# Queries and keys saved and stacked by halves, and the keys' projection moved ahead of y2's second half

## The reference, cut to what matters

```
x = x + L0(gn(x))      # gn: group norm in 32 groups of 4 channels, no affine
x = x + L1(gn(x))

L0: router: softmax over mean and std of the image -> 2 of 8 experts
    shared = silu(group_norm(conv1x1(x, 8 groups)))
    expert_k = silu(group_norm(conv3x3(x, w[chosen k], 8 groups))) * weight_k
    return shared + expert_1 + expert_2
L1: q, k, v = qkv_w @ x + qkv_b            # per pixel, 128 -> 3 * 128
    windows of 8 x 8 pixels (64 tokens), 8 heads of 16 channels
    attn = softmax(q k^T / 4 + bias[head])
    o = attn @ v + depthwise_conv7x7(v)
    return proj_w @ o + proj_b
```

## Time and profile before

| | |
|---|---|
| median of three runs | 932.93 us |
| the profiled execution | 934.59 us |
| its span | 932.9 us |
| TensorE busy | 743.6 us, 80% |
| VectorE busy | 578.1 us, 62% |
| ScalarE busy | 457.7 us, 49% |
| GpSimd busy | 197.0 us, 21% |
| clock granted to TensorE, mean | 0.879 |

### The profile page before, as it was taken

How to read it: one execution, slowest core, us unless ns; L and a number is a source line. 1 busy time by engine, 2 the same in 40 slices (tenths; PEclk the granted TensorE clock), 3 DMA queues, 4 the chain that set the end, 5 groups by cost and what they waited for, 6 DMA issues and landing times.

```text
span 932.9 us, 18414 instructions
## 1 busy us (share of the span) xinstructions
PE 743.6 (80%) x6926; PEld 422.7 (45%) x6926; DVE 578.1 (62%) x1136; ACT 457.7 (49%) x746; POOL 197.0 (21%) x289
## 2 busy tenths in 40 slices
PE   6143768888888989888989887979797989978785
PEld 5121334454545554545454545454545456534321
DVE  4724456675767666767676757575757587632296
ACT  1204546555555564646464646464646465344422
POOL 3122123131213140403130313131313020000044
PEclk9976969797979797979888988888988989999999
DMA  9224444545464545455554545454546254586435
GB/s 353 106 71 116 139 113 146 145 128 156 144 178 136 163 148 150 150 153 165 142 170 128 173 136 173 123 173 120 177 132 177 67 176 132 161 276 217 156 157 203
DMA packets 84046, 145.29 MB, mean 156 GB/s; under 512 B 24179, under 2 KB 48886, under 8 KB 83958
## 3 DMA queue, kind: packets, MB, share of 16 engines
q1 hardware_dynamic: 58102, 100.89, 34.8%
q0 software_dynamic: 21248, 25.36, 10.9%
q10 hardware_dynamic: 4608, 17.86, 5.2%
HBM read 84.21 MB, written 51.41 MB: 145 GB/s over the span
## 4 chain that ended last, share of the span: by engine, by line
PE 41%; DMA 19%; DVE 16%; ACT 8%; issue 7%; SPq 6%; POOL 1%; POOLq 1%; ACTq 0%; DVEq 0%
PE g L1061 11%; DMA sk_d<-khl 10%; PE g L1057 5%; PE g L1079 4%; PE t L1127 4%; DMA stack<-sk_d 3%; SPq L298 3%; ACT xw L540 3%; PE s L1116 3%; PE pv L1142 3%; DMA vt<-x 3%; PE t L1241 2%; PE s L1112 2%; SPq L292 2%; PE s L1241 2%
## 5 line engine op out<-in xcount | busy, mean ns | idle before, releaser
L806 DVE BATCH_NORM_STATS2 st<-y 128x6 f32<-128x512 f32 x96 | 66.6, 694 | 147.6 <-ACT y L522 147.6
L522 ACT ACTIVATE y<-g 128x512 f32<-128x512 f32 x96 | 57.2, 596 | 167.0 <-PE g L1061 87.0
L1061 PE MATMUL g<-xsh,wsel 96*128 96x512 f32 x256 | 127.8, 627 | 14.0 <-DMA xsh<-xs 10.5
L595 ACT ACTIVATE pt<-t 128x512 f32<-128x512 f32 x128 | 76.2, 597 | 118.8 <-PE t L1127 112.2
L870 DVE TENSOR_REDUCE mx<-s 128x8 f32<-128x512 f32 x128 | 87.8, 686 | 69.6 <-PE s L1116 69.6
L1127 PE MATMUL t<-ident,less 128*128 128x128 f32 x512 | 97.6, 321 | 3.7 <-DVE less L874 3.7
L1142 PE MATMUL pv<-vp,pt 128*64 128x34 f32 x2048 | 95.2, 242 | 5.0 <-ACT pt L595 4.8
L1112 PE MATMUL s<-bias,ident 128*128 128x512 f16 x128 | 56.7, 443 | 52.9 <-DMA stack<-sk_d 52.8
L1142 PEld LDWEIGHTS pv<-vp,pt 128*64 128x64 f32 x2048 | 80.1, 154 | 31.4 <-issue 25.0
L874 DVE TENSOR_TENSOR less<-s,mx 128x512 f32<-128x512 f32 x128 | 88.5, 692 | 4.4
L1079 PE MATMUL g<-xw,w 128*128 128x512 f32 x128 | 66.7, 640 | 15.4 <-ACT y L522 11.7
(11 more groups left out here) (159 smaller groups left out, 1158.5 us busy)
## 6 DMA issues: line engine op xcount, KB each, us to landing
xsh<-xs POOLq DMA_DIRECT2D x64, 210.0 KB, 5.4
stack<-sq_d SPq DMA_DIRECT2D x96, 128.0 KB, 3.1
stack<-sk_d SPq DMA_DIRECT2D x192, 64.0 KB, 2.8
xs<-xn ACTq DMA_DIRECT2D x16, 578.0 KB, 2.9
vt<-x SPq DMA_DIRECT2D x4, 2048.0 KB, 17.7
xin<-x POOLq DMA_DIRECT2D x16, 512.0 KB, 5.8
acc_d<-xr SPq DMA_DIRECT2D x16, 512.0 KB, 5.5
sq_d<-qhl SPq DMA_DIRECT2D x16, 512.0 KB, 7.7
```

The source lines that it names most:

```text
L522: act.activation(y[:, k, h * HALF:(h + 1) * HALF], g[h][:, :], ACT.Identity).then_inc(g_free[h], 1)
L595: act.activation(pt[:, p % 2].rearrange("p i w n -> p (i w n)"), tbk[p % 2][:, :], ACT.Exp).then_inc(sem["exp_done"], 1)
L806: last = v.bn_stats(st[:, 2 * k + h, :], y[:, k, h * HALF:(h + 1) * HALF])
L1061: last = mm(g[h][:, :], wsel[:, k - 1, C * dy:C * dy + C], xsh[:, k - 1, dy + 16 * h:dy + 16 * h + 16, 0:W], start=(dy == 0), stop=(dy == 1))
```

## The change

q and k get a semaphore for each half of the pixels. `save_half` saves one half (256 KB) when its own bank has been read, and for j > 0 when that half's stacks of the image before have landed. `stack_q` and `stack_k` take the place of `stack_qk`; each waits for its own half's save. In a step of SP the order becomes: q saved in two halves, q's first half stacked, k saved in two halves, k's first half stacked; later q's and k's second halves stacked. ScalarE waits by halves before it overwrites qhl and khl. On TensorE, ScalarE, VectorE and in `bank_uses` the keys of image b + 1 at p = 3 now come before y2 (1) of image b + 2; in bank 1 the order becomes q, k, y2 (1).

```diff
@@ bank_uses
         if has1:
             use("q", b + 1)
+        if has1:
+            use("k", b + 1)
         if has2:
             use("y2", b + 2, (1,))
-        if has1:
-            use("k", b + 1)
@@ SP
+            def save_half(j, half, name, dst, src, saved):
+
+                cols = slice(HALF * half, HALF * half + HALF)
+                sp.wait_ge(g_free[half], bank_ready(name, j, half))
+                if j:
+                    sp.wait_ge(stacked[half], STACK * j)
+                sp.dma_start(dst.rearrange("t c n -> c t n")[:, :, cols], src[:, :, cols]).then_inc(saved[half], 16)
+
             def save_q(j):
-
-                sp.wait_ge(g_free[1], bank_ready("q", j, 1))
-                sp.wait_ge(g_free[0], bank_ready("q", j, 0))
+                for half in range(2):
+                    save_half(j, half, "q", sq_d, qhl, q_saved)
+
+            def save_k(j):
+                for half in range(2):
+                    save_half(j, half, "k", sk_d, khl, k_saved)
+
+            def stack_q(j, half):
+
                 if j:
-                    sp.wait_ge(sem["stacked1"], STACK * j)
-                sp.dma_start(sq_d.rearrange("t c n -> c t n"), qhl[:, :, :]).then_inc(sem["q_saved"], 16)
...
+                    sp.wait_ge(sem["s_ready"], PAIRS * (j - 1) + PAIRS // 2 * (half + 1))
+                sp.wait_ge(q_saved[half], 16 * j + 16)
                 cols = slice(HALF * half, HALF * half + HALF)
                 for part, t in enumerate((0, 1, 0)):
                     sp.dma_start(qs[QD * part:QD * part + QD, :, cols],
                                  sq_d[t, :, cols].rearrange("(i c) n -> c i n", i=Q)).then_inc(stacked[half], 16)
+
+            def stack_k(j, half):
+
+                if j:
+                    sp.wait_ge(sem["s_ready"], PAIRS * (j - 1) + PAIRS // 2 * (half + 1))
+                else:
+                    sp.wait_ge(sem["setup_pool"], 1)
+                sp.wait_ge(k_saved[half], 16 * j + 16)
+                cols = slice(HALF * half, HALF * half + HALF)
                 for part, t in enumerate((0, 0, 1)):
...
                 if has1:
                     save_q(b + 1)
+                    stack_q(b + 1, 0)
                     save_k(b + 1)
-                    stack_qk(b + 1, 0)
+                    stack_k(b + 1, 0)
                 if b:
                     save_acc(b - 1)
                 load_x1(b)
                 if has1:
-                    stack_qk(b + 1, 1)
+                    stack_q(b + 1, 1)
+                    stack_k(b + 1, 1)
@@ ScalarE, high_qk
-                act.wait_ge(sem[used], 16 * b)
                 for h in range(2):
+                    act.wait_ge(used[h], 16 * b)
@@ TensorE, step (the same on ScalarE and VectorE)
                     if p == 3:
+                        if has1:
+                            project_qk(b + 1, 1)
                         if has2:
                             convolve(b + 2, 2, (1,))
-                        if has1:
-                            project_qk(b + 1, 1)
```

More of the change, by code:

```diff
@@ L129 @@
 rstd_done coef_scale coef_shift coefs_done silu_done sum_shared sum_first xr_done
-xw_done xr_saved x1_loaded q_hi k_hi q_saved k_saved stacked0 stacked1
+xw_done xr_saved x1_loaded q_hi k_hi q_saved0 q_saved1 k_saved0 k_saved1 stacked0 stacked1
 v_turned v_hi vt_done vt_saved s_ready s_max less_done turned exp_done pv_done
@@ L236, in program @@
         xin_loaded = [sem["xin_loaded0"], sem["xin_loaded1"]]
+        q_saved = [sem["q_saved0"], sem["q_saved1"]]
+        k_saved = [sem["k_saved0"], sem["k_saved1"]]
         stacked = [sem["stacked0"], sem["stacked1"]]
@@ L264, in _ @@
                 sp.dma_start(xall[:, 4 * n:4 * n + 4, :], xb[:, 4 * n:4 * n + 4, :]).then_inc(x_loaded[n], 16)
-            def save_q(j):
-                sp.wait_ge(g_free[1], bank_ready("q", j, 1))
-                sp.wait_ge(g_free[0], bank_ready("q", j, 0))
-                if j:
-                    sp.wait_ge(sem["stacked1"], STACK * j)
-                sp.dma_start(sq_d.rearrange("t c n -> c t n"), qhl[:, :, :]).then_inc(sem["q_saved"], 16)
-            def save_k(j):
[L276 to L284, removed]
+            def save_half(j, half, name, dst, src, saved):
[4 more added lines that the diff above has]
+                sp.dma_start(dst.rearrange("t c n -> c t n")[:, :, cols], src[:, :, cols]).then_inc(saved[half], 16)
+            def save_q(j):
+                for half in range(2):
+                    save_half(j, half, "q", sq_d, qhl, q_saved)
+            def save_k(j):
+                for half in range(2):
+                    save_half(j, half, "k", sk_d, khl, k_saved)
+            def stack_q(j, half):
                 if j:
                     sp.wait_ge(sem["s_ready"], PAIRS * (j - 1) + PAIRS // 2 * (half + 1))
-                elif half == 0:
-                    sp.wait_ge(sem["setup_pool"], 1)
+                sp.wait_ge(q_saved[half], 16 * j + 16)
                 cols = slice(HALF * half, HALF * half + HALF)
@@ L357, in _ @@
             save_k(0)
-            stack_qk(0, 0)
-            stack_qk(0, 1)
+            for half in range(2):
+                stack_q(0, half)
+                stack_k(0, half)
             save_xr(1)
@@ L544, in high_qk @@
             def high_qk(b, n):
-                dst, col, name, used, hi = ((qhl, BQ, "q", "q_saved", "q_hi"), (khl, BK, "k", "k_saved", "k_hi"))[n]
-                act.wait_ge(sem[used], 16 * b)
+                dst, col, name, used, hi = ((qhl, BQ, "q", q_saved, "q_hi"), (khl, BK, "k", k_saved, "k_hi"))[n]
                 for h in range(2):
+                    act.wait_ge(used[h], 16 * b)
                     act.wait_ge(g_ready[h], bank_ready(name, b, h))
@@ L621, in step @@
                     if p == 3:
+                        if has1:
+                            high_qk(b + 1, 1)
                         if has2:
                             copy_y(b + 2, 2, (1,))
-                        if has1:
-                            high_qk(b + 1, 1)
                     if p == 5:
@@ L944, in step @@
                     if p == 3:
+                        if has1:
+                            low_qk(b + 1, 1)
                         if has2:
                             y_stats(b + 2, 2, (1,))
-                        if has1:
-                            low_qk(b + 1, 1)
                     if p == 4 and b:
```

## The result

Slower by 0.9%: 938.8 us (median of 5, 937.29 to 941.59) against 929.92 (median of 5 beside it, 928.82 to 933.0), ratio 1.009 with interval 1.0061 to 1.0119. The forecast was 935.0, 0.2% above the median that it started from. The profiled execution took 941.59 us with a span of 939.7, 6.8 more than the span before.

What follows compares the result with a forecast made beforehand. The wait for key stacks sits in each image's first stretch; TensorE bounds the second. Earlier stacks -21.0 us and the swap +23.1 sum to +2.1, giving 935.0 on the median; range 914 to 952 for 8 in 10.

Steps and rivals of the forecast that it cites:

- The stall is worth 1.50 per step, not 3.8.: First stretch, 14 steps: without TensorE's wait for key stacks it falls from 19.37 to 17.87 us, -21.0 us in all.
- Line 841 would pay for GpSimd's subtraction in every step.: VectorE's residual sum: takes 2.95 instead of 1.28 us beside GpSimd's value split, giving back 1.67 of 3.1 gained.
- The stacks land early enough.: Key stacks in the example image: last landing at 346.8, before the limit of 349.0, so no cost.
- harmless limit: First stretch: stacks landing 11.2 us into it, as in step 11, still leave a stretch of 18.00 us.
- The swap costs 1.65 per step.: TensorE, y2's second half waits for VectorE to read the keys from the shared bank: 14 x 1.65 = +23.1 us.
- rival 2: TensorE's new 1.6 us gap drops the clock in half the images: +22 us, 957; chance 9%.
- Without an earlier landing nothing much would change.: Wait for stacks: the swap's shift of 1.65 us alone takes as much off it as the earlier landing.
- The sum: Whole kernel: -21.0 from the first stretches and +23.1 from the swap give +2.1 us.
- the forecast's own range: Whole time if the forecast holds: 929 to 941 us, forecast given 50%.
- Rivals 3 and 4: 3: line 841 not stretched, 20 us less, 915, chance 13%. 4: clock stays up, 35 less, 900, 8%.
- rival 1: Key stacks land late, beyond 349.0, behind SP's wait for q's save: 949, up to 962; chance 20%.

Runs made afterwards that it cites:

- split_k_first: Halves without the swap (old engine order), and on SP both halves of k saved before q's first half is stacked: ratio 0.982 to the kernel before, 0.9831 when rerun.
- no_read: The changed kernel with GpSimd's subtraction in split_v replaced by a memset of zeros that reads nothing: ratio 0.9955 to the kernel before.
- after_k_first: The changed kernel with both halves of k saved on SP before q's first half is stacked: ratio 1.007 to the kernel before.
- swap_only: The kernel before with only the keys' projection moved ahead of y2's second half, saves and stacks whole: ratio 1.0192 to the kernel before.
- split_only: The changed kernel with saves, stacks and semaphores by halves, but y2's second half before the keys again: ratio 0.9915 to the kernel before.
- y2_late: The changed kernel with y2's second half moved into part 4, behind the scores and values: ratio 0.9929 to the kernel before.
- split_k_first_sub: Halves without the swap, k saved before q's stacks, and GpSimd's subtraction held until the residual sums are done: ratio 0.9814 to the kernel before.

## Why the prediction was right or wrong

- *The stall is worth 1.50 per step, not 3.8.* Right in 13 steps: 17.81 to 18.10 each, against 17.87 forecast from step 13 of the kernel before. In all -18.6 instead of -21.0; the missing 2.5 are step 0, which has 20.40 because TensorE begins it at a granted clock of 0.50. (`split_k_first` has 20.12 there for another reason: a wait of 3.84 us for the stacks.)
- *Line 841 would pay for GpSimd's subtraction in every step.* Right in 13 of 14 steps (1.84 to 2.95 us; in step 10 the subtraction is over when the sum starts): median 2.81 instead of 1.28, VectorE's busy time up by 18.8 us (578.1 to 596.9). `no_read` takes it away.
- *The stacks land early enough.* Right, by `after_k_first`. In step 4 they land 9.9 into the stretch (350.90 - 340.96); the sum had 9.0 (346.8 - 337.8) and the harmless limit 11.2. q's first save takes 6.67 and k's 6.77 there, near the 6.5 that I took. For k this is the exception: its first half lands in 2.6 to 4.5 us in 10 of the 13 steps with row loads. In step 3 it takes 3.27, but then the stacks take 8.3 from the first issue to the last landing instead of my 4.5, and the two together are 11.6 against my 11.0. So in such a step the landing came out right by two errors that cancel. TensorE's scores start 8.2 to 10.8 us into the stretch in steps 1 to 13.
- *The swap costs 1.65 per step.* Right in kind, a little small: 23.0 / 13 = 1.77. The wait itself is 1.72.
- *The new gap could drop the clock (rival 2, 9% for half the steps).* It happened once, in step 0 of the profiled execution. The stretch with the wait grew by 3.5 instead of 1.65, and the first stretch behind it has the 2.5 above: 4.3 us in all. `no_read` repeats it (the clock falls 1.1 us after the same wait of 1.72 in step 0), and in `after_k_first` it falls about 7 us after it; `swap_only` with 1.66 keeps 1.00 there. The kernel before, `split_only` and `split_k_first` have no such wait and keep 1.00 up to their wait for the stacks; `y2_late` has none either, but falls behind another wait, of 2.25 us. So the fall comes behind a wait, not always behind this one; why only in step 0 stays open. I had this in a rival and nothing for it in the sum.
- *Without an earlier landing nothing much would change.* Wrong. The step that failed is the sentence that the shift of 1.65 takes as much off the wait as the halves do. `swap_only` has 8.3 us more in the first stretches than the change and a ratio of 1.019. The change was not 2% slower because the halves work.
- *The sum.* +2.1 forecast, +6.8 in the spans: +2.4 from the first stretches, +1.6 from 13 swaps (0.12 each) and +1.8 from step 0, less 0.9 behind the last step and 0.2 ahead of step 0. So 4.3 of the 4.7 us that were missing in the spans are that one fall of the clock. The medians differ by 8.9; the further 2 us are within the spread of the executions, and no term of mine explains them. The two large terms were right in kind and size; that their small difference came out with the right sign is partly luck, for the forecast's own range (929 to 941) reached to both sides of no change. Rivals 3 and 4 did not come true, and rival 1 neither.

## What to carry to other kernels

A wait's total is an upper bound that says little: look for one iteration in the trace in which the wait happens to be absent, and measure the whole stretch there. Moving a producer forward moves whatever it passes backward; a consumer that then shares its buffer needs other work of the same length between them, here 1.7 us of scores. And order the queue itself first: one line on SP, which took the keys' save out from behind the queries' landing, turned a 0.9% gain into 1.8%, where the swap of the engines' order cost 1.8%. The same line was worth nothing on the changed kernel, where another bound lay behind it.

## What the runs showed of the hardware that I had not expected

- What a save takes depends on its place against GpSimd's loads of expert rows more than on its bytes. Issued behind them it is slow: 7.0 to 8.9 us for 512 KB (before), 6.3 to 7.6 for the 256 KB of q's halves (after). Issued ahead of them it is fast: k's first half took 2.6 to 4.5 us in the ten steps in which its issue came 0.1 to 1.1 us ahead of the next row loads, 6.8 and 7.0 in the two in which it came 0.2 behind, and 8.2 in the one in which it came 2.5 behind. k's second halves, issued 0.5 us later, took 3.5 to 10.2. A whole save of q that came 0.3 ahead (before, at 511.55) took 2.8, as without row loads (2.7 to 2.9). Steps 3 and 4 of the changed kernel, k's first save and the row loads beside it:

```profile
293.22 3.27 DMA sk_d<-khl
293.86 1.27 POOL L435 DMA_DIRECT2D xsh<-xs  x2 [0.16 <-issue]
...
339.64 6.77 DMA sk_d<-khl
339.47 1.27 POOL L435 DMA_DIRECT2D xsh<-xs  x2 [0.16 <-issue]
```

- Two kernels with the same work in a stretch differed by 0.7 us a step by the granted clock alone (0.93 and 0.89, one execution each); a gain ahead of the clock's rise can be lost again behind it.
- VectorE's one-column product at line 798 took 0.69 instead of 0.16 us while GpSimd's late subtraction ran (305.70 and 304.25 in `split_k_first_sub`) and ended with it, at 306.39 and 306.38: small operations are held up too. It goes the other way as well: GpSimd's cast (line 436, before) takes 1.04 us at 101.81, where VectorE does nothing, and 1.89 at 345.44, behind VectorE's first residual sum (345.24 to 346.43).
